# Second attention: positions added to the queries by GpSimd in place instead of by two identity products on TensorE

## The reference

```python
q = (x @ Wq + bq).reshape(Bsz, Tlen, NUM_HEADS, HEAD_DIM)
...
q = q + pe[None, None, :, :]
k = k + pe[None, :, :]
scores = jnp.einsum('bhqd,bkd->bhqk', q, k) * scale
```

## Time and profile before

| what | value |
|---|---|
| median of 3 runs | 730.55 us (729.79 to 736.21) |
| profiled execution, its own time | 729.45 us |
| its span, from first to last instruction | 727.6 us |
| PE busy | 636.8 us, 88% |
| DVE busy | 531.4 us, 73% |
| ACT busy | 417.7 us, 57% |
| POOL busy | 251.3 us, 35% |
| second attention | about 258 us to 501 us of the span |

### The profile page before, as it was taken

The page is one execution under the profiler, slowest core; times in us unless marked ns, Lnnn a source line. Parts: engine busy times, 40 slices in busy tenths (PEclk is TensorE's granted clock), DMA queues, the critical chain, the costliest instruction groups (busy, mean ns, idle before and its releaser), DMA issues. The chain is left out here.

```text
span 727.6 us, 11182 instructions
## 1 busy us (share of the span) xinstructions
PE 636.8 (88%) x3414; PEld 450.1 (62%) x3414; DVE 531.4 (73%) x791; ACT 417.7 (57%) x869; POOL 251.3 (35%) x195
## 2 busy tenths in 40 slices
PE   3889999999999885988999999997788789988675
PEld 1667777777769753545566666665437778887223
DVE  5774434444445223278999999999999889999998
ACT  1365656556545354567778778875656566656310
POOL 0102212122200043000423542461115867787873
PEclk9799999999999998999999999999899999999888
DMA  8500000000059921022688998899862455554113
GB/s 278 201 5 9 12 12 7 11 7 8 26 161 294 323 58 30 1 68 61 157 201 191 219 237 218 201 228 262 196 149 80 148 150 163 153 144 117 37 43 83
DMA packets 61676, 89.99 MB, mean 124 GB/s; under 512 B 7712, under 2 KB 36256, under 8 KB 61632
## 3 DMA queue, kind: packets, MB, share of 16 engines
q1 hardware_dynamic: 41472, 57.96, 25.9%
q0 software_dynamic: 9408, 26.22, 17.3%
q10 hardware_dynamic: 10752, 5.24, 2.4%
HBM read 54.67 MB, written 14.81 MB: 95 GB/s over the span
## 5 line engine op out<-in xcount | busy, mean ns | idle before, releaser
L1645 DVE TENSOR_REDUCE nmax<-PS 128x1 f32<-128x128 f32 (+7 forms) x128 | 96.2, 751 | 110.5 <-PE PS L1046 96.0
L708 ACT COPY ROOM<-PS 128x512 f32<-128x512 f32 (+1 forms) x192 | 86.0, 484 | 101.3 <-PE PS L1058 92.0
L1074 PE MATMUL PS<-ROOM 128*128 128x512 f32 (+3 forms) x384 | 142.8, 491 | 0.5 <-ACT ROOM L708 0.5
L715 ACT ACTIVATE ROOM<-PS,nmax 128x128 f32<-128x128 f32 (+7 forms) x128 | 95.8, 749 | 30.9 <-DVE nmax L1645 28.6
L1058 PE MATMUL PS<-CST,ROOM 128*128 128x128 f32 x576 | 87.3, 280 | 12.1 <-ACT ROOM L708 10.4
L570 POOL DMA_DIRECT2D ROOM<-ROOM x32 | 28.6, 893 | 181.9 <-DVE ROOM L1744 181.9
L1058 PEld LDWEIGHTS PS<-CST,ROOM 128*128 128x128 f32 x576 | 65.8, 144 | 33.9 <-issue 26.2
L1074 PEld LDWEIGHTS PS<-ROOM 128*128 128x128 f32 x384 | 65.5, 192 | 29.9 <-issue 26.3
L1043 PE MATMUL PS<-LATER 128*128 128x512 f32 (+2 forms) x192 | 74.5, 498 | 7.4 <-ACT ROOM L715 5.9
L535 POOL DMA_INDIRECT rows_in<-XN,slot x48 | 70.8, 1474 | 27.5 <-DVE slot L1545 14.2
L549 POOL TENSOR_TENSOR QL<-ROOM,QH 128x512 fp32r<-128x512 f32 x16 | 20.6, 1287 | 155.2 <-ACT QH L683 155.2
(11 more groups left out here) (182 smaller groups left out, 1214.2 us busy)
## 6 DMA issues: line engine op xcount, KB each, us to landing
ROOM<-bc_rows SPq DMA_DIRECT2D x32, 512.0 KB, 4.2
ROOM<-ROOM POOLq DMA_DIRECT2D x32, 512.0 KB, 5.6
LATER<-in_w SPq DMA_DIRECT2D x48, 256.0 KB
ROOM<-in_w SPq DMA_DIRECT2D x32, 321.0 KB, 4.3
rows_in<-zero SPq DMA_DIRECT2D x20, 256.0 KB, 3.3
X<-GA POOLq DMA_DIRECT2D x12, 256.0 KB, 7.5
LATER<-rows_in SPq DMA_DIRECT2D x24, 128.0 KB
rows_out<-ROOM ACTq DMA_DIRECT2D x24, 128.0 KB
```

The lines of the kernel that those rows point to most:

```text
L708: nc.scalar.copy(dst, src).then_inc(s_ed, 1)
L715: nc.scalar.activation(PR[:, s, 0:nk], sc[:, 0:nk], ACT.Exp, bias=nmax[:, i % 4:i % 4 + 1], accum_out=rsum[:, i:i + 1]).then_inc(s_ex, 1)
L1074: r = mm(PS[:, 6, lo:BANK], V[:, j, :], PT[:, 4 * group + j, lo:BANK], start=j == 0, stop=True, skip_group_check=True)
L1645: nc.vector.tensor_reduce(nmax[:, i % 4:i % 4 + 1], sc[:, 0:(i + 1) * P], AX_X, ALU.max, negate=True).then_inc(s_nm, 1)
```

## The change

PE no longer adds the positions. ACT writes projection plus bias to `Q1` as before, and GpSimd then adds `peT` to the half in place and raises `s_qe`, on which PE (and SP) now wait. The split parts `PEH`, `PEL` and the converted identity go away.

```diff
             def query(g, h, b, hf):
                 r = mm(bank(7), wq[:, h % 2 if isinstance(h, int) else parity[0], :],
-                       XNT[...], start=True, stop=b == 0)
-                if b:
-                    if isinstance(g, int) and g == HEADS:
-                        pe.wait_ge(s_pel, 1)
-                    mm(bank(7), identr[:], PEH[:, hf * BANK:(hf + 1) * BANK], start=False, stop=False)
-                    r = mm(bank(7), identr[:], PEL[:, hf * BANK:(hf + 1) * BANK], start=False, stop=True)
+                       XNT[...], start=True, stop=True)
                 r.then_inc(s_qp, 1)
...
+            def query_placed(g, hf):
+
+                pool.wait_ge(s_qr, 2 * g + hf + 1)
+                sl = slice(hf * BANK, (hf + 1) * BANK)
+                nc.gpsimd.tensor_tensor(Q1[:, sl], Q1[:, sl], peT[:, sl], ALU.add).then_inc(s_qe, 1)
...
             def attention_second():
+                query_placed(HEADS + 1, 0)
                 for t in range(TB, NT):
                     gather(0, 0, t, GA[:, t, :], s_g0[1])
+                query_placed(HEADS + 1, 1)
+                query_placed(FIRST, 0)
                 heads = 2 * HEADS - FIRST
                 for h in range(heads):
                     n = 2 * h
                     y_add(n, 0)
+                    query_placed(FIRST + h, 1)
                     y_add(n, 1)
                     x_add(FIRST + h - 1, 0)
                     if h == 0:
                         pool.wait_ge(s_slot, 2)
                     scatter(1, range(TB * h // heads, TB * (h + 1) // heads))
                     y_add(n + 1, 0)
+                    if h + 1 < heads:
+                        query_placed(FIRST + h + 1, 0)
                     y_add(n + 1, 1)
                     x_add(FIRST + h - 1, 1)
...
             attention_first()
+            query_placed(HEADS, 0)
             for i in range(2):
                 pool.wait_ge(s_mo[0][i], 16 * (QUADS // 2))
             for t in range(TB):
+                if t == 2:
+                    query_placed(HEADS, 1)
                 gather(0, 0, t, GA[:, t, :], s_g0[0])
             attention_second()
...
-            nc.scalar.copy(PEH[:], peT).then_inc(s_peh, 1)
...
-                s_query = s_qr if b else s_qe
-                pe.wait_ge(s_query, 2 * g + 1)
+                pe.wait_ge(s_qe, 2 * g + 1)
...
-                        pe.wait_ge(s_query, 2 * g + 2)
+                        pe.wait_ge(s_qe, 2 * g + 2)
...
-                        sp.wait_ge(s_qr, 4 * HEADS)
+                        sp.wait_ge(s_qe, 4 * HEADS)
...
-            cp(identr[:], ident)
...
-                tt(PEL[:], peT, PEH[:].bitcast(F32), ALU.subtract).then_inc(s_pel, 1)
```

More of the change, by code:

```diff
@@ L84, in sem @@
             return ctx.enter_context(nc.semaphore(name))
-        with ExitStack() as second_half_of_XN:
-            second_half_of_XN.enter_context(nc.sbuf_tensor("under_PEH", [P, 3 * T], F32))
-            PEH = second_half_of_XN.enter_context(nc.sbuf_tensor("PEH", [P, T], F32R))
         X = sb("X", [P, NT, D])
@@ L138, in build @@
         HEAD_END, MOE_END, END = 53 * KB, 90 * KB, 133 * KB
-        identr = sb("identr", [P, P], F32R)
         with ExitStack() as first_split:
-            PEL = first_split.enter_context(nc.sbuf_tensor("PEL", [P, T], F32R))
-            first_split.enter_context(nc.sbuf_tensor("under_KH", [P, END - T], F32))
+            first_split.enter_context(nc.sbuf_tensor("under_KH", [P, END], F32))
             KH, KL, QH, QL = (first_split.enter_context(nc.sbuf_tensor(n, [P, T], F32R)) for n in ("KH", "KL", "QH", "QL"))
@@ L268, in build @@
         s_xo = [sem(f"weighted_output_added{s}") for s in range(2)]
-        s_peh = sem("positions_high_ready")
-        s_pel = sem("positions_low_ready")
         s_mw = [sem(f"expert_weights{i}") for i in range(4)]
@@ L1011, in query @@
                 r = mm(bank(7), wq[:, h % 2 if isinstance(h, int) else parity[0], :],
-                       XNT[:, b * T + hf * BANK:b * T + (hf + 1) * BANK], start=True, stop=b == 0)
-                if b:
-                    if isinstance(g, int) and g == HEADS:
-                        pe.wait_ge(s_pel, 1)
-                    mm(bank(7), identr[:], PEH[:, hf * BANK:(hf + 1) * BANK], start=False, stop=False)
-                    r = mm(bank(7), identr[:], PEL[:, hf * BANK:(hf + 1) * BANK], start=False, stop=True)
+                       XNT[:, b * T + hf * BANK:b * T + (hf + 1) * BANK], start=True, stop=True)
                 r.then_inc(s_qp, 1)
@@ L1624, in values @@
                        bc(bv, 1, 4), ALU.add).then_inc(s_ve, 1)
-            def positions_low():
-                dve.wait_ge(s_peh, 1)
-                tt(PEL[:], peT, PEH[:].bitcast(F32), ALU.subtract).then_inc(s_pel, 1)
             keys(0)
@@ L1799, in result @@
                        W4[w][:, :, 4 * P + 2:4 * P + 2 + D], ALU.add).then_inc(s_my[0], 1)
-                positions_low()
                 result(0, 0, 0, None)
```

## The result

The changed kernel took 728.16 us (median of 20 runs, 724.26 to 735.43), the kernel before, in the same measurement, 733.94 us (20 runs, 729.4 to 737.66). The ratio is 0.9925, with a 95% interval of 0.9905 to 0.9946. In this measurement the change makes the kernel 0.75% faster, where 735.4 us, 0.7% slower, was forecast. The time lies within the range given, but on the other side of no change. The profiled execution took 727.74 us, with a span of 725.9.

A forecast was written before the change was run, and what follows sets the result against it. PE was taken to set the pace of heads 10 to 15, DVE 1.34 us behind. Terms -0.1 + 0.6 + 0 + 1.85 + 2.5 = +4.9 us on 730.55 gave 735.4 us; range 726 to 745.

The forecast's parts named there:

- I take 0 for it: Head 8, DVE and ACT idle over 8 us during the gathers: no change assumed, ends -7 and +5.6 us.
- The second rival: Head 8: GpSimd stops its gathers, so DVE's and ACT's long wait closes; -2.1 us, 728.5 us, chance 0.15.
- eight gathers still follow: Head 8: the argument given against that unexplained wait closing (-7 us) when GpSimd interrupts its gathers.
- The third rival: Head 8: the unexplained wait keeps its distance to the last gather and grows; +10.5 us, 741.1 us, chance 0.18.
- Head 8 without the hole: Head 8, first query half on the path through GpSimd's add: +0.6 us, bounds 0 and +1.4.
- The handover: Head 8: GpSimd's 1.27 us add and passing the half on make PE's first scores about 0.9 us later.
- Head 9: Two GpSimd adds delay DVE operations, about +0.85 and +1.0: +1.85 us, bounds 0 and +2.5.
- Heads 10 to 15: Adds hold up DVE's recurrences, so DVE sets the pace: +2.5 us, bounds -4.6 and +14.0.
- the sum of 25.28: Steady head: DVE's 23.45 us busy plus 0.93 and 0.90 lost to adds, above PE's 23.87 us.
- Head 15: No next query, so only one add and little waiting for PE: +0.9 us.
- Head 12: Four scatters; one add falls under a maximum reading PSUM, with no loss taken: 24.38 us, -0.4 us.
- The first and the fourth rival: GpSimd does not hold DVE: -4.1 us, 726.4, chance 0.12; adds hold DVE full length: +10.6 us, 741.2, chance 0.15.

The follow-up runs named there:

- its variant where no hole is: Changed kernel with GpSimd's add for half 0 of head 9 moved behind batch 1's eight gathers, against the kernel before: 726.97 us, ratio 1.0107.
- the pause alone: Kernel before plus one GpSimd wait ahead of the second eight gathers, no adds, against the kernel before: 721.05 us, ratio 0.9872.
- the early pause: Kernel before plus one GpSimd wait after two gathers, until ACT has half 1 of head 8 out: 718.97 us, ratio 0.9998; in a later group 730.03 us, 0.9987.
- the third measurement of the changed kernel: Changed kernel, unaltered, measured again in the last group against the kernel before: 728.23 us, ratio 0.9952.
- the reading passes: Kernel before plus 11 unused GpSimd passes that read SBUF, at the adds' places in heads 10 to 15: 731.82 us, ratio 1.0024.
- the writing ones: Kernel before plus 11 unused GpSimd memsets, which only write, at the adds' places in heads 10 to 15: 729.54 us, ratio 0.9993.
- The shifted code: Kernel before plus 96 empty instructions at the start of ACT's and DVE's programs, against the kernel before: 732.47 us, ratio 1.0013.

## Why the prediction was wrong

**The step that failed** is "I take 0 for it", on the hole in head 8. The two ends kept beside it were -7 and +5.6. From the last expert product to XN the kernel before took 35.94 us, the changed one 29.43; the whole hole is worth 10.9 us there, and the changed kernel takes as long as its variant where no hole is (28.97). The second rival, the gathers stop and the hole closes, had the mechanism. It had a chance of 0.15, and against it stood "eight gathers still follow". That objection was wrong: in the kernel with the pause alone eight gathers follow as well, to 284.2, and of the hole 4.1 us on the path remain. What counts most is where the run of sixteen is broken: eight and eight (the changed kernel: two, six and eight) lose the hole or most of it, and the kernels with two and fourteen keep it.

That this rival's 728.5 us lies so near the measured 728.16 is luck twice. It took 7 for a hole of 10.9 and +0.6 for a loss in head 8 of about 4, and the two errors cancel. And it was added to 730.55, while the kernel before had a median of 733.94 in the measurement that decided. The third rival, which tied the hole's end to the last gather, falls with it.

The general error was to take the middle for a wait that no row explains. A wait of 8 us on the path, with its inputs long there, was the largest single quantity within reach of the change, larger than the sum of all the terms worked out. The change moved just the thing that ran beside it. Equal bounds on both sides are no reason for 0.

**Head 8 without the hole** was mis-sized. The prediction took +0.6, bounds 0 and +1.4. The handover came as worked out: PE's first scores start 3.99 us after the last expert product (261.61 - 257.62), and 3.11 us (260.08 - 256.97) in the kernel with the early pause without the hole; that is the forecast 0.9. But by XN, where no hole is, the add's variant is 28.97 - 25.08 = 3.9 us behind. Two things make most of it, and the prediction priced neither.

The first is the clock. Busy time and clock from 262 to 267 us, changed kernel:

```profile
262.00:267.00 5.00, 5.00 (x13) 2.75 (x13) 0.90 (x3) 1.71 (x5) 2.46 (x3) 0.50 0.10 26
```

PE stood 2.12 us and was then granted half speed, 1.2 of 2.4 GHz, for these 5 us: 13 records where the kernel before has 22 in the same stretch, at clock 1.00. In the variant without the hole the clock is 0.83 from 257 to 267. In the third measurement of the changed kernel it stays at 1.00 after the same 2.12 us of waiting. The maximum over 896 columns, counted from the last expert product, starts at 14.2 us in that trace, just as in the kernels with unchanged query and no wait ahead of it; at 15.7 in the variant without the hole; and at 17.0 in the first trace of the changed kernel. So up to this place the full clock gives the handover back, since two products less follow it, and the lower clock costs 1.5 to 2.8 us.

The second are the gathered rows. The prediction let the first eight gathers end 2.4 us later and put no price on it. In the variant without the hole DVE waits for the rows of batch 0, and in the kernel with the early pause alone it does not:

```profile
275.10 2.19 DVE L1816 SCALAR_TENSOR_TENSOR X<-GA,wsel,X 128x128 f32<-128x128 f32 x8 [1.78 <-DMA GA<-rows_out,slot]
```

```profile
272.33 2.19 DVE L1823 SCALAR_TENSOR_TENSOR X<-GA,wsel,X 128x128 f32<-128x128 f32 x8
```

The 1.5 and the 1.8 us leave 0.6 of the 3.9, and PE is at half clock once more from 281 us on.

**Head 9** was right in place and kind, +1.4 for +1.85. The timeline of the changed kernel:

```profile
311.86 2.28 DVE L1841 SCALAR_TENSOR_TENSOR ROOM<-ROOM 128x2048 f32<-128x2048 f32 x1
...
313.20 2.06 POOL L548 TENSOR_TENSOR LATER<-LATER,ROOM 128x512 f32<-128x512 f32 x1 [26.86 <-ACT LATER L696]
327.17 1.27 POOL L548 TENSOR_TENSOR LATER<-LATER,ROOM 128x512 f32<-128x512 f32 x1 [11.91 <-ACT LATER L696]
...
314.65 2.77 DVE L1845 TENSOR_TENSOR ROOM<-ROOM 128x2048 f32<-128x2048 f32 x1
...
327.33 1.14 DVE L1546 TENSOR_SCALAR slot<-rs 128x8 uint32<-128x8 f32 x1
```

The first pass itself waits for DVE's product that began at 311.86 (2.06 us instead of 1.27), and then holds the next by 0.49. The second catches an operation of eight columns, which takes 1.14 us instead of 0.17. The hold works in both directions, and not only against operations with two SBUF inputs: this one has one input.

**Heads 10 to 15** were right in mechanism, +3.2 for +2.5. By the starts of the first maximum, heads 10 to 14 last 25.22, 25.04, 25.94, 25.04 and 25.03 us, before 24.74, 24.78, 24.72, 24.80 and 24.80. The four steady ones lost 1.2 us together and not 2.0. In a steady head the two held recurrences take 3.09 and 3.25 us, 1.78 more than 2.28 each, where 1.83 was forecast; but DVE's records overlap by about 0.1 us where it does not wait, and two waits are gone, so the sum of 25.28 was too long by 0.24. Head 15 gave +0.8 for +0.9. Head 12, with its four scatters, was put at -0.4 and cost +1.2. "Inside a recurrence that ends at 414.1" didn't hold, since in the heads before it the work had moved. The timelines of POOL, DVE and PE there:

```profile
410.66 1.65 POOL L548 TENSOR_TENSOR LATER<-LATER,ROOM 128x512 f32<-128x512 f32 x1
...
410.89 2.50 DVE L1740 TENSOR_TENSOR ROOM<-ROOM 128x1024 f32<-128x1024 f32 x1
...
412.43 0.48 PE L1045 MATMUL PS<-LATER 128*128 128x128 f32 x2 [1.41 <-POOL LATER L548]
```

The add came down on a product with two SBUF inputs, 2.50 us for 1.21, and the half was late: PE waited 1.41 us. A position to 0.5 us can't be carried over four heads whose length changes.

**The first and the fourth rival.** That GpSimd does not hold DVE up is refuted by the reading passes against the writing ones. That it holds DVE for its full length each time did not happen either; a head stayed at 25.04, below the 25.5 named. The Trainium skill (SBUF — State Buffer, "Who interferes with whom") is borne out: a reading pass and an operation with two SBUF inputs exclude each other, and a GpSimd instruction that only writes does not hold such an operation. The same section names tensor_scalar among the operations that can take both of DVE's ports, so one SBUF input is not always safe. The prediction passed over that; the slot operation above, a tensor_scalar, waited for 0.97 us, and the trace agrees with the section, not with the prediction's shorter version of it.

**The whole.** Without the hole the estimate's sign is right and its size too small: +4.9 forecast, +7.8 measured in the nearest kernel (one add stands elsewhere in it). With the hole, closing it is worth more than that: the pause alone measured -8.5 us (721.05 for 729.57).

**Open.** What the engines wait for. The fetch of instructions was named with the second rival (the Trainium skill, Runtime: NRT & Kernel Launch, "Instruction fetch mechanics"). What the runs show speaks against it, without closing it. The shifted code has the hole where it was. And the profiles list packets of instructions: in the kernel before none falls between 248.2 and 287 us, so none in or just before the hole. The kernel with the reading passes has one at 268.2 us, 19 us earlier, and its waits are 8.27 and 8.51 us for 8.21 and 8.46. Whether this list holds the fetches of every engine is not known. Nor is it known why in one group the waits were absent from every trace. A pause at other places, or gathers further apart, was not tried. The 1.0 us of the last line of the table above was not followed: that stretch takes 223.5 to 225.7 us in the five traces with all sixteen adds and 222.8 to 224.2 in the others.

## What to carry to other kernels

When a wait that nothing explains lies on the path and the change touches what runs beside it, that wait is a term of the sum, and the cheapest experiment is to touch only that neighbour: here one wait instruction of GpSimd that splits sixteen gathers in two was worth 1.3% and the change around it 0.4 to 0.75%. A GpSimd pass that reads SBUF takes about 0.9 us from a DVE that is already full when it lies just ahead of an operation with two SBUF inputs, and less than 0.1 us where it lies under a maximum that reads PSUM. So work moved there from TensorE pays up to DVE's idle time, and its place counts beside its amount. A change that wins should be taken apart as one that loses; its gain may come from a side effect. And a label in a profile is an inference: in this case several microseconds of the same wait stand under another engine's name, and the start of the same instruction in a kernel without the wait shows it.

## What the hardware showed that was not expected

- A run of 14 to 16 indirect gathers 1.25 us apart went with 7 to 25 us of waits labelled remote on ACT and DVE, some 7 to 11 us of them on the path; two runs of eight with 3.9 us between them left 2.75 us so labelled and 4.1 us on the path. In one group of four no such wait appeared, and the same kernel took 719.2 instead of 730 us, on a chip that showed it in another group.
- A GpSimd pass of 128x512 delayed even an 8-column DVE operation with one SBUF input by 0.97 us, and was itself stretched from 1.27 to 2.06 us by a DVE product in progress. A memset inside a recurrence took 0.92 us and left the recurrence at 2.28.
- After a wait of 2.12 us PE was granted 0.50 for the next 5 us in one execution of the changed kernel, and 1.00 after the same wait in another execution of the same kernel.
